# One 512 KB spread per scan slot instead of two of 256 KB, in a hybrid scan, attention and FFN kernel

## The reference

```python
x_in = jnp.einsum('bsd,de->bse', x, w_in)
proj = jnp.einsum('bsd,dp->bsp', x_in, w_x)
dt_low, Bm, Cm = jnp.split(proj, [DT_RANK, DT_RANK + D_STATE], axis=-1)
dt = softplus(einsum('bsr,rd->bsd', dt_low, w_dt) + b_dt) * (DT_MAX - DT_MIN) + DT_MIN
A = -jnp.exp(A_log)                      # 256 channels x 16 states
def step(h, inp):                        # over the 512 tokens
    dtt, ut, bt, ct = inp
    dA = dtt[:, :, None] * A
    barA = jnp.exp(dA)
    inp_term = jnp.einsum('bdn,bn,bd->bn', dA, bt, ut)
    h = barA * h + inp_term[:, None, :]
    y = jnp.einsum('bdn,bn->bd', h, ct) + Dp * ut
```

## Time and profile before

| | us |
|---|---|
| median of 3 runs | 2286.72 (2280.93 to 2288.96) |
| the profiled execution, its own time | 2287.08 |
| its span, first to last instruction | 2285.4 |

### The profile page before, as it was taken

One profiled execution on the slowest core, in us unless ns is written; L12 is line 12 of the kernel. 1 busy time (PEld: TensorE's weight loads), 2 busy tenths in 40 slices (PEclk: granted clock), 3 DMA queues, 4 the chain that ended last, 5 costly groups with the idle time before them and its releaser, 6 DMA issues. The chain is left out here.

```text
span 2285.4 us, 40569 instructions
## 1 busy us (share of the span) xinstructions
PE 2030.1 (89%) x12780; PEld 1290.7 (56%) x12844; DVE 2011.9 (88%) x3843; ACT 1865.5 (82%) x3544; POOL 1246.9 (55%) x1837
## 2 busy tenths in 40 slices
PE   2548899898989999898999999899999989989997
PEld 0215556465655646565565656656565655647574
DVE  6898997989989898998989899898989999897745
ACT  4779888797979889797988979798898979867463
POOL 6224464555646555564655556465555646564754
PEclk8569999999999999999999999999999999999999
DMA  3442322323232232323223232322323232331000
GB/s 88 111 128 75 93 56 70 88 75 84 60 97 58 71 89 74 86 61 93 58 70 88 74 84 59 96 58 71 88 75 87 59 94 58 91 76 36 6 6 12
DMA packets 104450, 165.97 MB, mean 73 GB/s; under 512 B 15458, under 2 KB 34094, under 8 KB 104238
## 3 DMA queue, kind: packets, MB, share of 16 engines
q1 hardware_dynamic: 104238, 163.37, 26.9%
HBM read 146.55 MB, written 16.78 MB: 71 GB/s over the span
## 5 line engine op out<-in xcount | busy, mean ns | idle before, releaser
L1718 DVE TENSOR_TENSOR_SCAN scan_bufs<-scan_bufs,inp_bank 128x512 f32<-128x512 f32 x512 | 614.0, 1199 | 30.4 <-ACT scan_bufs L1117 28.9
L1434 PE MATMUL bank<-w_gu,f_xqT 128*128 128x512 f32 x1024 | 468.8, 601 | 3.4 <-ACT f_xqT L1180 3.4
L1449 PE MATMUL bank<-w_dn,f_hqT 128*128 128x256 f32 x1536 | 364.2, 389 | 25.2 <-ACT f_hqT L1180 23.8
L1111 ACT ACTIVATE scan_bufs<-scan_bufs,a_rows 128x512 f32<-128x512 f32 x512 | 367.6, 725 | 9.8 <-DMA scan_bufs<-dt_copy 9.5
L1728 DVE TENSOR_TENSOR scan_bufs<-scan_bufs,c_bank 128x512 f32<-128x512 f32 x512 | 341.7, 667 | 1.7
L1449 PEld LDWEIGHTS bank<-w_dn,f_hqT 128*128 128x128 f32 x1536 | 292.1, 194 | 89.1 <-issue 38.0
L1434 PEld LDWEIGHTS bank<-w_gu,f_xqT 128*128 128x128 f32 x1024 | 190.3, 192 | 220.2 <-issue 210.7
L1006 POOL TENSOR_TENSOR f_h<-f_h,f_h_scale 128x704 f32<-128x704 f32 x128 | 179.7, 1404 | 224.5 <-DVE f_h L1598 224.5
L1017 POOL TENSOR_TENSOR f_h<-f_h,f_h_lean 128x704 f32<-128x704 f32 x128 | 218.5, 1707 | 109.0 <-DVE f_h L1779 81.4
L1117 ACT ACTIVATE scan_bufs<-scan_bufs 128x1024 f32<-128x1024 f32 x256 | 271.2, 1059 | 1.4
L1006 POOL TENSOR_TENSOR f_h<-f_h,f_h_inv 128x704 f32<-128x704 f32 x128 | 177.7, 1389 | 114.5 <-DVE f_h_inv L1613 111.5
(11 more groups left out here) (197 smaller groups left out, 4331.5 us busy)
## 6 DMA issues: line engine op xcount, KB each, us to landing
scan_bufs<-dt_copy SPq DMA_DIRECT2D x512, 256.0 KB, 3.9
xp<-L_attn_a_x SPq DMA_DIRECT2D x16, 512.0 KB, 4.2
dt_copy<-dt SPq DMA_DIRECT2D x32, 256.0 KB, 3.4
out<-x SPq DMA_DIRECT2D x64, 128.0 KB, 3.5
w_attn<-L_attn_b_W_attn SPq DMA_DIRECT2D x1, 768.0 KB, 4.5
masked_scores<-L_ffn_w_gate SPq DMA_DIRECT2D x1, 704.0 KB
masked_scores<-L_ffn_w_up SPq DMA_DIRECT2D x1, 704.0 KB
f_h<-L_ffn_w_down SPq DMA_DIRECT2D x2, 352.0 KB, 10.8
```

The lines of the kernel that those rows point to most:

```text
L1111: nc.scalar.activation(half, half, ACT.Exp, scale=a_rows[:, c, at:at + 1]).then_inc(root_ready, 1)
L1434: last = nc.tensor.matmul(to[:, :], f.xqT[:, k, :], w_gu[:, k, g, lo:hi], start=(k == 0), stop=(k == DH - 1))
L1449: last = nc.tensor.matmul(to[:, 0:D], f.hqT[:, k, :], w_dn[:, k, :], start=(k == 0), stop=(k == FK - 1))
L1718: nc.vector.tensor_tensor_scan(half, half, inp[:, :], 0.0, ALU.mult, ALU.add)\
```

## The change

Both halves of a slot come with one DMA of 512 KB. For that, the copy in HBM has a new layout, (batch, 128-channel half, slot, 8 channels, 2 x 512): the rows of the two halves of a slot lie beside each other, so that one partition's 4 KB are contiguous. The copy of dt is written by four DMAs of 32 partitions each for h = 0 and four for h = 1, eight for a batch; all four count on `dt_kept[h]`. The five pairs of semaphores `dt_spread` become five. Both decays of a slot wait for the same landing. Orders and computation stay as they are.

```diff
-        dt_spread = [[sem(f"dt_spread{i}_{h}") for h in range(DH)] for i in range(SLOTS)]
+        dt_spread = [sem(f"dt_spread{i}") for i in range(SLOTS)]
-        dt_copy = nc.dram_tensor("dt_copy", (NB, DH, P, T), F32, kind="Internal").ap()
+        dt_copy = nc.dram_tensor("dt_copy", (NB, DH, NS // DH, 8, DH * T), F32, kind="Internal").ap()
@@ keep_dt
-                sp.dma_start(dt_copy[b, h], dt[:, h, :]).then_inc(dt_kept[h], 16)
+                for j in range(4):
+                    to = dt_copy[b, h].rearrange("(q i) e (s t) -> q i e s t", i=2, s=DH)
+                    sp.dma_start(to[:, j // 2, :, j % 2, :], dt[32 * j:32 * j + 32, h, :]).then_inc(dt_kept[h], 16)
@@ spread_dt
-                    sp.wait_ge(dt_kept[k // (NS // DH)], upto(b, 1, 0, 16))
+                    sp.wait_ge(dt_kept[k // (NS // DH)], upto(b, 1, 0, 4 * 16))
-                for h in range(DH):
-                    if nth:
-                        sp.wait_ge(dt_spread[slot][h], 16 * nth)
-                        sp.sem_inc(dma_allowed, 1)
-                    c, rows = rows_of(DH * k + h)
-                    lo = 8 * rows
-                    sp.dma_start(bar[slot][:, h, :], dt_copy[b, c, lo:lo + 8, :].unsqueeze(0).broadcast_to([NS, 8, T]))\
-                        .then_inc(dt_spread[slot][h], 16)
+                if nth:
+                    sp.wait_ge(dt_spread[slot], 16 * nth)
+                    sp.sem_inc(dma_allowed, 1)
+                c, pair = divmod(k, NS // DH)
+                sp.dma_start(bar[slot].rearrange("p h t -> p (h t)"),
+                             dt_copy[b, c, pair].unsqueeze(0).broadcast_to([NS, 8, DH * T]))\
+                    .then_inc(dt_spread[slot], 16)
@@ decay, on ACT
-                act.wait_ge(dt_spread[slot][h], 16 * (nth + 1))
+                act.wait_ge(dt_spread[slot], 16 * (nth + 1))
@@ part_p, on ACT
-                        act.wait_ge(dt_kept[h], upto(b - 1, 1, 0, 16))
+                        act.wait_ge(dt_kept[h], upto(b - 1, 1, 0, 4 * 16))
```

## The result

| us | before | after |
|---|---|---|
| median, 20 runs each, taken in turn | 2284.41 (2280.65 to 2288.96) | 2290.44 (2286.42 to 2293.66) |
| the profiled execution, its own time | 2287.08 | 2293.03 |
| its span | 2285.4 | 2291.3 |

The changed kernel takes 1.0024 times the time of before, with a 95% interval of 1.0017 to 1.0032. It is a little slower, inside the 0.3% of the forecast. The times of one kernel spread over some 10 us (before lies at 2280 to 2290 us, with many times near either end), and the median of before alone came out between 2284.41 and 2288.43 us in the five sets of runs of this case. So ratios are compared here, each taken against the runs of before beside it; they are not the quotients of the medians.

A forecast was written before the change was run, and what follows sets the result against it. PE and DVE together were taken to set the pace, DMA counting only where an engine waits for a landing. Terms of 0 to 6.7 us, taken as 1.5, gave 2288.2 us in terms of the 2286.72 median; range 2277.5 to 2298.

The forecast's parts named there:

- Issues on SP are worth nothing: SP's queue: one issue (0.52 us) and one wait saved per slot, worth nothing because SP is ahead and idles.
- When a slot lands: Spreads: 512 KB land about 4.5 us after the first issue, 5.8 us behind a load of x.
- The faster rival: Spreads run at the load's 400 GB/s, slots land 0.7 us sooner, at most down to 2277.6 us; chance 0.10.
- the choice of 2.0 us: Transfer time taken for a 512 KB spread in a burst, against 1.3 us at 400 GB/s.
- Batches 3 to 8, slot 3: 0, with cover left: First decay late by 0.5 to 1.0 us, covered by ACT's idle time before f_xqT; cost 0, 0.6 us cover left.
- The slower rival: Slot 3 lands past its cover, at least 0.6 us later than today's second half; 2300 us, chance 0.14.
- Batches 9 to 13: the first decay is later than the second landing anyway: Slot 3 there: the first decay already starts after the second half's landing, so cost 0.
- Batch 2, slot 3: 0 to 0.95 us: The copy of yT behind the first decay, and PE's work with it, come up to 0.95 us later.
- Batch 14: 0 to 0.6 at slot 3, up to 0.5 at slot 5: At slot 3 the square and f_xqT follow without idle time, 0 to 0.6 us; slot 5 up to 0.5.
- Batch 1: 0 to 4.1, taken at 0.5: Slots 3 and 7 late by 0 to 1.0 and 0 to 1.3 us; copy in pieces 0 to 1.8, taken at 0.5.
- The sum: All terms over the whole kernel: 0 to 6.7 us, taken as 1.5 us because delays partly cover each other.
- ACT waits 10 to 20 us: ACT's idle time for spreads over the span was to go from 9.5 us to 10 to 20 us.

The follow-up runs named there:

- e5_wait_for_both: The kernel before, both halves still spread by 256 KB DMAs; only each slot's first decay also waits for the second half: ratio 1.0001, 2286.38 us.
- e3_copy_on_32_rows: The changed kernel, copy's slots reordered in memory so each piece writes 32 rows in one dimension instead of 4 x 8: ratio to before 1.0000, 2286.27 us.

## Why the prediction was right, and where it was not

The forecast was 2288.2 and within 0.3%. The measured median is 2290.44; on the 2286.72 from which the forecast started, the three ratios are 2289.5 to 2292.2. The mechanism that it gave for a cost, the first decay of slot 3 that waits for the second half, is the one that the traces show in batch 2, and in one of three traces of after in batch 14. Some of the agreement is luck: what the sum lacked in batch 14 (up to 2.7 us) and what batches 9 to 13 gave back (1.1 to 1.5 us) go against each other. Step by step:

- *Issues on SP are worth nothing.* Right: 256 fewer, at 0.51 us, and no gain.
- *When a slot lands.* For slot 3, behind the load of x, the prediction said 5.8 us, for an undisturbed one 4.5. Line 889 in batch 5 of after, slots 3 and 4, then 5 and 6, and what DMA moves in the second burst:

```profile
L889 SPq DMA_DIRECT2D scan_bufs<-dt_copy x2: 514/539/564, 672.4 to 673.1; - x2
...
DMA to landing us min/median/max: 6.0/6.6/7.2
...
L889 SPq DMA_DIRECT2D scan_bufs<-dt_copy x2: 514/514/515, 681.1 to 681.8; - x2
...
DMA to landing us min/median/max: 4.4/5.1/5.8
...
DMA packets 252, 0.93 MB, mean 252 GB/s; under 512 B 24, under 2 KB 24, under 8 KB 252
```

  6.0 and 4.4 us. The median over all is 5.1, not the 4.7 forecast, as the second slot of a burst lands after 5.8 to 7.2. Rows of 4 KB move at 252 GB/s in 682.8 to 686.5 us, no faster than the 277 of a burst of before (678.5 to 681.5, the stretch of the earlier trace rows) and the 253 of another (671 to 674). The faster rival falls with that, and the choice of 2.0 us, made against the 400 GB/s of the load, holds.
- *Batches 3 to 8, slot 3: 0, with cover left.* Right in the sum, short in the size. ACT in batch 5, answering to the earlier trace rows:

```profile
677.08 0.38 ACT L1181 ACTIVATE yT<-bank 128x256 f32<-128x256 f32 x1 [1.59 <-PE bank L1539]
678.37 1.33 ACT L1112 ACTIVATE scan_bufs<-scan_bufs,a_rows 128x512 f32<-128x512 f32 x2 [0.91 <-DMA scan_bufs<-dt_copy]
679.99 0.38 ACT L1181 ACTIVATE f_xqT<-bank 128x256 f32<-128x256 f32 x1 [0.28 <-PE bank L1419]
```

  f_xqT had 1.11 us of idle time before it, and has 0.28; I had said 0.6. The others keep 0.20 to 0.63. The slower rival, which by the prediction needed 0.6 us more, would have needed 0.2 to 0.6: it was nearer than I made it.
- *Batches 9 to 13: the first decay is later than the second landing anyway.* Wrong. They wait 0.74 to 1.09 us now. The late yT that held the first decay back there was the work of the five falls of the clock, and these are gone. The slack that I read from one trace belonged to a clock that the trace of after does not have. It cost nothing: these batches take the 133.03 us of the table.
- *Batch 2, slot 3: 0 to 0.95 us.* 1.3 to 1.4 us in each of three traces, the wait itself 3.32 instead of 2.00. The link to yT holds; the term was mis-sized, and it left out that eight matmuls behind it take 0.8 us more at the lower clock.
- *Batch 14: 0 to 0.6 at slot 3, up to 0.5 at slot 5.* This is the term that failed: 3.3, 1.7 and 1.6 us in the three traces. In the first of them the first link was right (f_xqT late with no idle time to cover it); in the two others ACT doesn't wait for slot 3, the clock falls in w_dn ahead of it, and no term of the sum stands for that. What is missing in the first is the second link: a longer stand of PE, a lower clock, 1.6 us more in eight matmuls, a sum another 2.3 us late and with it slot 5. The sum of terms had only the landing, and not what follows when the engine that waits last is PE.
- *Batch 1: 0 to 4.1, taken at 0.5.* 0: DVE's shift from 73 to 212 us is -0.07. SP, ACT and DVE there, answering to the earlier trace rows:

```profile
133.89 2.56 SPq L874 DMA_DIRECT2D dt_copy<-dt  x4
139.18 2.12 SPq L889 DMA_DIRECT2D scan_bufs<-dt_copy  x2
...
144.07 1.33 ACT L1112 ACTIVATE scan_bufs<-scan_bufs,a_rows 128x512 f32<-128x512 f32 x2 [3.89 <-DMA scan_bufs<-dt_copy]
...
148.98 1.21 DVE L1719 TENSOR_TENSOR_SCAN scan_bufs<-scan_bufs,inp_bank 128x512 f32<-128x512 f32 x1
```

  The spread follows the copy by 5.3 us instead of 3.8, 1.5 us more, near the lower bound of 1.2 and far from 4.2. ACT waits 3.89 us instead of 1.47, and the scan starts 2.7 us later on the clock of a trace that was already 3.0 us late at 45 us: no delay of its own. That DVE is saturated there was the cover, and it held. 

  By the rule of the Trainium skill that the prediction cites ("DMA: Bandwidth & Descriptors") the term would have been 1.8. The runs agree with it in so far as the shape shows in the issue and in the time from there to the first spread (above), and not with the price that I had hung on it.
- *The sum.* 1.5 us forecast; the traces show 3.0, 2.6 and 0.7 between 212 and 2130 us, as +1.3 in batch 2, +1.6 to +3.3 in batch 14 -1.1 to -1.5 in batches 9 to 13, and from 0.0 to -1.4 between 1890 and 2130. The three ratios stand for 2.7 to 5.5 us. What is missing between the two isn't settled: it would lie ahead of 212 us or behind 2130, where traces of the same kernel differ by 2.7 us and more, and no run here separated these. Nor do the ratios of e5_wait_for_both (1.0001) and e3_copy_on_32_rows (1.0000) confirm the cost, though both have the two steps. So the steps and, in batch 2, their cause are shown; that they are the whole of the measured 0.12 to 0.24% is not.
- *ACT waits 10 to 20 us* was forecast; 29.7, 28.9 and 27.1 were found, because batches 9 to 13 joined (4.6 us), batches 0 and 1 took some 5 us more, and slot 3 landed 0.1 to 0.5 us later than its second half before. *Period unchanged* was right.

Not tried: giving PE other work in its idle time of batch 14, which would show the price of the lower clock by itself, without any wait for a spread.

## What to carry to other kernels

Two transfers made into one arrive when the later one did; where the consumer can start on the first half, look for the few places without slack, and follow each through to the engine that sets the pace, since 1.55 us of waiting at slot 3 of batch 14 stand at the head of a step of 3.3 us in one trace, and the waits in batches 3 to 13 cost nothing. The other find was in the same queue: a load that waits for its buffer held up two spreads whose buffers had been free for 8 us, and with it behind them the changed kernel takes 0.9990 of the time of before instead of 1.0012 to 1.0024. In an order written by hand, ask of each entry what is ready behind it.

## What was not expected of the hardware

A late landing can cost more than its own length where PE waits last: behind 2.58 us of idle time the granted clock went to half, and eight matmuls took 1.6 us more. Nor is the clock the same from one kernel to the next in the same place: behind 1.61 us of idle time it fell in batch 9 of before (4.51 us for twelve matmuls) and held in after (2.83). And 4 KB rows read 16 times over are no faster than 2 KB rows: 252 GB/s against 253 and 277 in two bursts, while the load of x, of the same size, ran at about 400.
